# A second set of gather slots and index tiles for the even and odd tiles of a graph layer

## The reference, cut to what matters

```python
def layer0(x, src, dst, w, W1, b1, W2, b2):
    msg = w[:, None] * x[src]                       # gather 412,500 rows of x
    agg = segment_sum(msg, dst, num_segments=N)
    h = relu((x + agg) @ W1 + b1)
    return h @ W2 + b2

def layer1(h, src, dst, w, attr, ...):
    h1 = h @ lin1_w.T
    c = 0.5 * (cos(w * pi / 10) + 1)
    f = softplus(attr @ nn_w1.T + nn_b1) - log(2)   # needs no node values
    W = (softplus(f @ nn_w2.T + nn_b2) - log(2)) * c[:, None]
    agg = segment_sum(W * h1[dst], src, num_segments=N)
    return (h1 + agg) @ lin2_w.T + lin2_b

x = layernorm(x + layer0(x, ...))
x = layernorm(x + layer1(x, ...))
```

## Time and profile before

| | us |
|---|---|
| median of 3 runs (9307.72 to 9319.87) | 9315.23 |
| the profiled execution | 9315.85 |
| its span, first to last instruction | 9314.2 |
| mean granted TensorE clock | 0.739 |
| PE / DVE / ACT / POOL busy | 6033.2 / 6494.6 / 3471.8 / 6297.2 |
| edge loop of layer 0, first to last gather issued | 158.0 to 4368.7 |

### The profile page before, as it was taken

How to read it: one execution, slowest core, us unless ns; L and a number is a source line. 1 busy time by engine, 2 the same in 40 slices (tenths; PEclk the granted TensorE clock), 3 DMA queues, 4 the chain that set the end, 5 groups by cost and what they waited for, 6 DMA issues and landing times. The chain is left out here.

```text
span 9314.2 us, 204001 instructions
## 1 busy us (share of the span) xinstructions
PE 6033.2 (65%) x35189; PEld 4808.1 (52%) x35190; DVE 6494.6 (70%) x20428; ACT 3471.8 (37%) x6781; POOL 6297.2 (68%) x6541
## 2 busy tenths in 40 slices
PE   2666666666666666666655556666666666666676
PEld 1444444444444444444444446666666666666665
DVE  7777777777777776665655556777777777777655
ACT  2333333333333333333544443333333333333202
POOL 2777777777777777775277777777777777777400
PEclk8676766776767667776855557888888888888887
DMA  3444444444444444444444446666666666666554
GB/s 101 148 146 147 148 144 146 149 146 143 146 149 147 145 145 148 149 147 142 143 134 134 134 134 199 208 210 206 205 206 208 209 207 206 205 207 207 174 167 147
DMA packets 803241, 1533.30 MB, mean 165 GB/s; under 512 B 193070, under 2 KB 206820, under 8 KB 802707
## 3 DMA queue, kind: packets, MB, share of 16 engines
q1 hardware_dynamic: 593415, 1093.58, 36.2%
q0 software_dynamic: 209456, 436.16, 15.7%
q10 hardware_dynamic: 348, 3.33, 0.1%
HBM read 967.92 MB, written 564.58 MB: 165 GB/s over the span
## 5 line engine op out<-in xcount | busy, mean ns | idle before, releaser
L1204 POOL DMA_INDIRECT sorted_messages<-rows,sidx x3224 | 3212.4, 996 | 1154.7 <-issue 932.4
L432 POOL DMA_INDIRECT xg<-x_rows,gidx x3224 | 3043.0, 944 | 1306.8 <-issue 1020.2
L475 PE MATMUL bank<-onehot,xg 128*128 128x42 f32 x6448 | 1116.6, 326 | 1400.4 <-DMA xg<-x_rows,gidx 1386.2
L475 PEld LDWEIGHTS bank<-onehot,xg 128*128 128x128 f32 x6448 | 1004.2, 233 | 1474.0 <-DMA xg<-x_rows,gidx 1457.1
L1132 PE MATMUL bank<-hot,block_rows 128*128 128x128 f32 x9312 | 1576.2, 347 | 145.4 <-DVE hot L1286 145.1
L1132 PEld LDWEIGHTS bank<-hot,block_rows 128*128 128x128 f32 x9312 | 1530.3, 260 | 169.2 <-issue 154.0
L481 PE MATMUL bank<-attr,nn 128*128 128x512 f32 x1612 | 1453.7, 1057 | 3.0 <-DVE hid L506 3.0
L1102 PE MATMUL bank<-w_nn2T,e_hid 128*128 128x128 f32 x6448 | 1039.0, 314 | 162.2 <-DMA e_hid<-hidden 162.1
L1102 PEld LDWEIGHTS bank<-w_nn2T,e_hid 128*128 128x128 f32 x6448 | 1007.8, 226 | 245.3 <-DMA e_hid<-hidden 212.1
L1113 PE MATMUL bank<-h1w,ohT 128*128 128x128 bf16 x3224 | 349.4, 275 | 1069.6 <-DVE ohT L1233 1066.4
L1257 DVE SCALAR_TENSOR_TENSOR rows<-filt,meta,bank 128x128 f32<-128x128 f32 x3224 | 904.7, 343 | 94.7 <-DVE filt L1248 47.2
(11 more groups left out here) (180 smaller groups left out, 7427.8 us busy)
## 6 DMA issues: line engine op xcount, KB each, us to landing
block_rows<-sorted_messages SPq DMA_DIRECT2D x389, 792.0 KB
hidden<-hid SPq DMA_DIRECT2D x404, 512.0 KB
e_hid<-hidden SPq DMA_DIRECT2D x403, 512.0 KB
sorted_messages<-zero SPq DMA_DIRECT2D x403, 264.0 KB
dstb<-dst SPq DMA_DIRECT2D x403, 256.0 KB
attr<-attr_cols SPq DMA_DIRECT2D x403, 204.0 KB
xg<-x_rows,gidx POOLq DMA_INDIRECT x3224, 4.2
sorted_messages<-rows,sidx POOLq DMA_INDIRECT x3224
```

Of the source, the lines that this page charges most:

```text
L432: pool.indirect_dma_start(xg[s][:, :], None, x_rows, bass.IndirectOffsetOnAxis(ap=gidx[s // HALF][:, s % HALF:s % HALF + 1], axis=0),).the ...
L475: nc.tensor.matmul(bank[0][:, 0:WIN], xg[s][:, :], onehot[:, s, :], start=(s == 0), stop=(s == SUB - 1)).then_inc(summed, 1)
L1204: pool.indirect_dma_start(table, bass.IndirectOffsetOnAxis(ap=sidx[b][h][:, s:s + 1], axis=0), rows[b][h][:, s, :], None).then_inc(landed[ ...
```

## The change

The slots for gathered rows (`xg`), the index tiles (`gidx`) and their semaphores (`gathered`, `gidx_ready`) get a second set. Even tiles use set 0, odd tiles set 1. ACT, POOL and PE run their loops over pairs of tiles with the body written twice (on PE in each of the four parts, with a single tile where a part begins on an odd or ends on an even one), and count for each set how many jobs it has had. A gather now waits for the matmul that last read its own set, two jobs back, and an index copy for the gathers of two jobs back. DVE's and SP's loops are as they were. The setup primes 16 semaphores rather than 8 by small DMAs.

```diff
-        gathered = [sem(f"gathered{s}") for s in range(SUB)]
+        gathered = [[sem(f"gathered{b}_{s}") for s in range(SUB)] for b in range(2)]
...
-                    for s in range(SUB):
-                        prime(pool, spare[s:s + 1, :], gathered[s], zero)
+                    for b in range(2):
+                        for s in range(SUB):
+                            prime(pool, spare[SUB * b + s:SUB * b + s + 1, :], gathered[b][s], zero)
...
-                gidx = [sb2(f"gidx{h}", [P, HALF], i32) for h in range(2)]
-                xg = [sb2(f"xg{s}", [P, D], f32) for s in range(SUB)]
+                gidx = [[sb2(f"gidx{b}_{h}", [P, HALF], i32) for h in range(2)] for b in range(2)]
+                xg = [[sb2(f"xg{b}_{s}", [P, D], f32) for s in range(SUB)] for b in range(2)]
...
ACT
-                        with act.Fori(0, T) as t:
+                        sent = RowTable(act, "act0")
+
+                        def tile(t, b):
+
                             windows = jobs.windows()
                             with act.Fori(0, windows):
-                                j = jobs.number()
                                 jobs.read_ahead(t)
                                 for h in range(2):
                                     for s in range(HALF * h, HALF * h + HALF):
-                                        act.wait_ge(gathered[s], 16 * (j + 1))
-                                    nc.scalar.activation(gidx[h][:, :], srci[:, ds(t * SUB + HALF * h, HALF)],
-                                                         ACT.Copy).then_inc(gidx_ready[h], 1)
+                                        act.wait_ge(gathered[b][s], 16 * (sent.number(b) + 1))
+                                    nc.scalar.activation(gidx[b][h][:, :], srci[:, ds(t * SUB + HALF * h, HALF)],
+                                                         ACT.Copy).then_inc(gidx_ready[b][h], 1)
                                 jobs.step()
+                                sent.step(b)
                             for h in range(2):
                                 soft_1(t, h)
+
+                        in_pairs(act, 0, T, tile)
...
POOL
-                                j = jobs.number()
+                                last_sum = pool.snap(after[b], min_val=0, max_val=MAXJOBS)
...
-                                        pool.wait_ge(gidx_ready[s // HALF], j + 1)
-                                    wait_apart(pool, summed, SUB * j + s + 1, passed)
+                                        pool.wait_ge(gidx_ready[b][s // HALF], sent.number(b) + 1)
+                                    wait_apart(pool, summed, SUB * last_sum + s + 1, passed)
...
                                 jobs.step()
+                                sent.step(b)
+                                pool.reg_mov(after[b], jobs.job)
+
+                        in_pairs(pool, 0, T, tile)
...
PE
-                                        pe.wait_ge(gathered[s], 16 * (j + 2))
-                                        nc.tensor.matmul(bank[0][:, 0:WIN], xg[s][:, :], onehot[:, s, :],
-                                                         start=(s == 0), stop=(s == SUB - 1)).then_inc(summed, 1)
+                                    pe.wait_ge(gathered[b][s], 16 * (sent.number(b) + 2))
+                                    nc.tensor.matmul(bank[0][:, 0:WIN], xg[b][s][:, :], onehot[:, s, :],
+                                                     start=(s == 0), stop=(s == SUB - 1)).then_inc(summed, 1)
```

More of the change, by code:

```diff
@@ L241, in _ @@
                     pool.wait_ge(s_b3, 16 * 9)
-                    for s in range(SUB):
-                        pool.wait_ge(gathered[s], 16)
+                    for b in range(2):
+                        for s in range(SUB):
+                            pool.wait_ge(gathered[b][s], 16)
                 @block.vector
@@ L421, in _, with tile @@
                         jobs = TileTable(pool, "pool0", nwin)
-                        with pool.Fori(0, T) as t:
+                        sent = RowTable(pool, "pool0")
+                        after = [pool.alloc_register(f"pool0_after{b}") for b in range(2)]
+                        for b in range(2):
+                            pool.reg_mov(after[b], 0)
+                        def tile(t, b):
                             windows = jobs.windows()
                             with pool.Fori(0, windows):
-                                j = jobs.number()
+                                last_sum = pool.snap(after[b], min_val=0, max_val=MAXJOBS)
                                 for s in range(SUB):
@@ L456, in _ @@
                         for q, first, past_last in parts:
                             plan_part(q)
[L458 to L468, removed]
-                                    pe.wait_ge(flushed, j + 2)
-                                    pe.wait_ge(onehot_ready, j + 1)
-                                    for s in range(SUB):
-                                        if s == HALF:
-                                            jobs.read_ahead(t)
-                                        pe.wait_ge(gathered[s], 16 * (j + 2))
-                                        nc.tensor.matmul(bank[0][:, 0:WIN], xg[s][:, :], onehot[:, s, :],
-                                                         start=(s == 0), stop=(s == SUB - 1)).then_inc(summed, 1)
-                                    jobs.step()
-                                for h in range(2):
-                                    pe.wait_ge(attr_in, 16 * (t + 1))
-                                    pe.wait_ge(hid_set, taken_up(t, h))
-                                    nc.tensor.matmul(bank[2 + h][:, :], nn1[:, :], attr[:, h, :], start=True, stop=True).then_inc(z1_set, 1)
@@ L483, in _ @@
+                            in_pairs(pe, first, past_last, tile)
                     @block.vector
```

31 lines of the change are left out of this document (27 added, 4 removed).

## The result

The changed kernel takes 9341.71 us (median of 10 runs, 9331.06 to 9351.23), the kernel before, run beside it, 9315.79 (9300.70 to 9330.61). The ratio is 1.0027, 95% interval 1.0018 to 1.0037: slower by 0.27%, 26 us, where no change was forecast. The profiled execution took 9341.08, 25 us more than that of before.

The account below looks back on a forecast made before the run. The prediction took a ring over two tiles (gather, matmuls, product, Abs/Exp/Ln, index copy, gather) as the bound. Its terms summed as 9315.85 - 1 - 8 + 9 = 9315.85, so 9315 us, no change; range 9290 to 9354.

Parts of the forecast that it names:

- The ring over two tiles: Gather, matmuls, product, Abs/Exp/Ln, index copy, gather: claimed as the bound, 12.11 us where POOL alone would need 11.25.
- the floor: POOL's own pace over the gather loop: 3223 x 1.25 = 4029 us, 182 us below the 4210.7 taken.
- rival A: The gathers' latency is the bound after all and POOL goes to its floor: 9134 us; chance 0.04.
- ACT's landing waits: ACT's waits for gathers before index copies: nothing hangs on them, so removing them gives 0, with -1 us for late landings.
- POOL's summed wait: POOL's waits for PE's matmul at four part starts, 25 us: 2.5 gained at three starts, 0.5 at the first, -8 us.
- POOL's pace then allows the next slot 0: After the second part start, the next tile's slot 0 could start at 1249.76, not 1252.5: 2.7 us gained.
- Register work on ACT: Instructions between last Ln and index copy: +0.09 us in even tiles' ring, -0.09 in odd; +9 us in all.
- the ring keeps its 12.1 us: The path from slot 7 of one tile to slot 0 of the tile after the next stays as long.
- first piece of 4.74 us: From slot 7's gather start to the start of the product of line 481, gather landing and PE's matmuls included.
- the rest: POOL's register instructions and eight more priming DMAs, 0 us each; SP, DVE and layer 1 not touched.
- Rival E: POOL's lead at part starts or another phase of gathers against SP transfers lengthens landings: 9356 us; chance 0.02.
- Rival C: Register work between ACT's waits is dear and the even tiles' ring leads: 9361 us; chance 0.15.

Follow-up runs that it names:

- The kernel with the ring cut: Changed kernel, with ACT making a tile's index copies ahead of the Abs, Exp and Ln of the tile before: 9138.77 us, ratio 0.9778.
- slots_only: Kernel before with two sets of `xg` but one of `gidx`, in the changed kernel's order; the index copy waits for the tile before: ratio 1.0002.
- indices_only: Kernel before with two sets of `gidx` but one of `xg`, in the old order: ratio 1.0032.
- act_slow: Kernel before, with each of ACT's four landing waits ahead of the first index copy made four times, every landing wait's number worked out anew: ratio 1.0132.
- act_pairs_only: Kernel before, with only ACT's loop written in pairs of tiles, body unchanged: ratio 0.9997.
- after_moved: Changed kernel plus 448 unused bytes per partition behind the index tensors, so attr and hidden begin on multiples of 512 again: ratio 0.9986.
- before, again: Kernel before, unchanged, profiled again on the chip of the follow-up runs: first to last gather 4237.1 us.
- before_moved: Kernel before plus 64 unused bytes per partition behind the index tensors, so slots, attr and hidden lie 64 bytes further on: ratio 1.0023.
- act_number_each: Kernel before with its plain loop, ACT working out the number to wait for anew ahead of each of its eight landing waits: ratio 1.0004.

## Why the prediction was wrong, and where it was right

1. **The ring over two tiles is the bound, and the floor lies 182 us below: right.** The kernel with the ring cut came to 9139, where rival A, with the same floor but the gathers' latency as its cause, had 9134. The Trainium skill (Trainium Kernel Development and Optimization, Best Practices) says to double-buffer; these runs agree once the copy stands ahead of the softplus, and not before.
2. **ACT's landing waits, -1 us: right in kind, too small.** 1357.7 us went and came back as 1229 us of wait for the product. But the stalls inside a tile fell from 34 to 18 us (33 to 20 in the second pair of profiles), and I had seen none of these 14 to 16. Most of the fall stands ahead of slot 5: seven stalls of 1.0 to 2.1 us before, 9 us in sum, and next to none after. They stay in slots_only, where the landing wait stays, and go in indices_only, where it goes.
3. **POOL's summed wait, -8 us: wrong.** The stalls at part starts moved one tile on and summed to 29.8 us in place of 26.0. The 41 tiles around the four starts took 452 us before and 455 to 458 with the change, so the term was +3 to +6. The step that failed is "POOL's pace then allows the next slot 0": with one more set POOL gets past the stall's old place, and the tile behind it pays.
4. **Register work on ACT, +9: the size may hold, the parts do not.** I took +0.09 for the even ring and -0.09 for the odd one; it is +0.23 and -0.01. By act_slow's rate half of the mean of 0.11 comes out, which gives the estimate of 11 us; the variants that take the work away or add it alone don't show it clear of noise. The Trainium skill (Advanced Engine Details and Errata, Control Flow Timing) gives a compare-and-branch about 108 ns; the runs show more for it together with an addition: in act_pairs_only the odd tiles lose both, and the stretch is shorter by 0.46 - 0.24 = 0.22. Ahead of even tiles, where the jump back is over a longer body, it is longer by 0.10.
5. **The step that failed and decided is "the ring keeps its 12.1 us".** It took the landing inside the ring's first piece of 4.74 us as given, and under "the rest" the place of the new tensors was put at nothing without a word. (Rival E had longer landings, at a chance of 0.02 and by another mechanism.) The new tensors moved the others by 64 bytes, landings of slot 7 grew by 0.1 to 0.2 us at the same distance, and that is +0.23% by itself and 0.41 to 0.47% between the changed kernel in its two layouts. The intervals of these two figures overlap, so whether it counts for more in the changed kernel stays open.
6. **With the layout held, the forecast of "no change" stands, in part by luck**: -0.14% (-0.24 to -0.04), 13 us where the sum had 0. Its terms of -1, -8 and +9 cancelled, and so do what came in their place: -13 us of stalls inside tiles in after_moved, +3 at the part starts and an estimated +11. So the 13 us are not accounted for. The profiles don't show them either: the loop of after_moved is 5 us longer than that of before, again. Rival C foretold the sign and fits the first profile well, 0.69 in even tiles and the even ring in the lead. But with all of C's instructions and the old layout (after_moved) nothing is lost, so C was not the cause.

## What to carry to other kernels

Before a second buffer is added, walk the ring that the first one sits in: if the buffer's refill stands behind other work in program order, move it ahead of that work first; here the second sets alone gave -0.1 to +0.3%, order alone -0.8%, order with a second set of indices -1.0%, and order with both second sets -2.2%. A delay put into a ring and a transfer halved tell more than taking small things away: one shows how much of a delay comes out, the other who makes it. And when a change adds tensors, give the old kernel the same layout before the loss is put down to instructions.

## What was new of the hardware

- The landing of 128 gathered rows depends on when another queue's load starts. With a load of 204 KB issued at 0, slot 5 or 6 starting in the half us ahead of it landed after 5.6 and 5.5 us, at 0 to 0.5 behind after 5.4 and 5.2, slot 7 at 2 to 2.5 behind after 3.7 (before, again); without half of that load slot 7 took 2.52 in the mean.
- 64 bytes of shift in SBUF: 0.1 to 0.2 us more per landing of slot 7 at the same distance behind the load, 0.23% of the program (before_moved).
- 12 waits on ACT, each with its number worked out anew, took 1.08 us, 0.09 each (act_slow beside act_number_each).
